# A fused two-layer kernel on Trainium2: one turn moved by a step, one normalisation moved ahead of a product, and the first gate given its own RMS factor

## The chip, the cores and the metric

The kernel runs on one core of a Trainium2 chip. One call computes both layers for all 32 batches. The metric is the device time of one call in microseconds (us). Each time comes from an execution on the chip; the profile is one further execution with the hardware profiler on.

## The reference, cut to what matters

x is 32 batches of 128 tokens with 128 features, all float32.

```python
# layer 0: RMS norm, gated MLP, 8-bit activations and ternary down weights
scale = cond @ norm_w.T + 1.0
ms = mean(x * x, -1)
h = x * (scale[:, None, :] * rsqrt(ms + 1e-6))
val, gate = split(h @ up_w.T, 2, -1)             # 512 each
h = val * gelu(gate)                             # exact gelu
y = act_quant(h) @ weight_quant(down_w).T
x = y + x
# layer 1: modulated attention (16 heads of 8) and modulated MLP
cond = silu(silu(t_embd @ W_t1.T + b_t1) @ W_t2.T + b_t2 + c_embd) @ W_c.T + b_c
g1, b1, g2, b2, a1, a2 = split(cond, 6, -1)
h = layernorm(x) * g1[:, None, :] + b1[:, None, :]
o = attention(h @ W_qkv.T + b_qkv) @ W_o.T + b_o
x = x + o * a1[:, None, :]
h = layernorm(x) * g2[:, None, :] + b2[:, None, :]
x = x + (gelu_tanh(h @ W_f1.T + b_f1) @ W_f2.T + b_f2) * a2[:, None, :]
```

## The kernel before, in words

The tokens of a batch lie on the 128 partitions, so one batch is a 128x128 tile of `x_tok`. Batches are taken in 8 groups of 4 (`GRP`). Nothing plans the order at run time: each engine's program is written out by hand, each engine takes its instructions in that order, and semaphores tie the engines together. Three stages follow each other and overlap at their seams.

- Stage A, `gated_mlp(s)`, is layer 0, one batch per step, with every engine a step or more behind the one before it. TensorE turns x (`transpose_x`), ScalarE multiplies the turned tile by the conditioning scale (`scale_x`, into `h0T`), TensorE makes the gate product and the val product (512 columns each), ScalarE takes Gelu with the RMS factor as its scale (`gate`, L772), VectorE multiplies val, RMS factor and gate (`hid`, L923). The RMS factor `rstd0` of four batches at once is made in two pieces: VectorE's `mean_squares` (`ms`, L870) and POOL's power -0.5 (`rms`, L1100). For the first group VectorE also makes the squares itself, at the start of its program: the first x comes in a load of its own, batches 1 to 3 in a second one. Then VectorE goes on to the weights of the down product: it sums |w| (`w_abs`, L879), TensorE adds the sums over the partitions (L286, 128x1), and four VectorE operations round the weights (`w_rnd`, `w_int`, `w_tern`, L887 to L891). `hid` of batch 0 is behind these in VectorE's order.
- Stage B, `attention(b)`, is the attention of one batch per step. In two halves of 8 heads TensorE makes scores (`exp_scores`), ScalarE exponentiates them (`exps`, L806), and TensorE weighs the values with the result (`weigh`). One step later VectorE turns the sums (`normalize`, `o_turn` L978, `rinv` L981), POOL divides (`scale_output`, `o_norm` L1190), VectorE turns the quotient back (`turn_back`, `feat` L985). In the last steps all exp scores use one pair of banks, so scores wait for the exp before them.
- Stage C, `mlp(i)`, is the output projection, the residual, the second layer norm and the MLP, one group per step. For a group: product with W_o (`output_projection`), VectorE's bias and gate (`gate_projection`, `projT`), the turn back to token rows (`residual`, L474), VectorE's addition into `x_tok` (`add_residual`, L999) and statistics (`statistics`, L1006 and L1010), POOL's `layer_norm` (`var_e`, `xc`, `rstd`, `xn`, L1196 to L1204), TensorE's turn of `xn` (`normalized_features`, L482), VectorE's `modulate` (`h2T`, L1017), four products with W_f1 each followed by ScalarE's Gelu (L845), and the product with W_f2.

The first pieces of stage C are put into the last attention steps. `FRONT` and `FRONT_END` (L87, L88) say which piece TensorE runs in which step: a piece of `FRONT` in the middle of the step, between the first weighing and the second scores, one of `FRONT_END` at its end. `FRONT_BANK` gives each its PSUM bank. Before, the turn of group 0's normalised rows ("norm", 0) is in the middle of step 30, the residual of group 1 ends step 30, the projection of group 2 ends step 31. Step 32 holds only what batch 31 still needs, and then `mlp(2)` begins, whose first products are the W_f1 products of group 0. VectorE's and POOL's counterparts are called from their own `attention(b)` (L1021) and `operand_parts(b)` (L1212): POOL runs `layer_norm(0)` at the end of step 29 and `layer_norm(1)` at the end of step 32, behind `scale_output(31)`.

Of the kernel before, what the change touches and what calls it, by code (L numbers as in the profile page):

```python
# [15 lines left out]
B = 32  # L16
D = 128
# [66 lines left out]

FRONT = {27: ("proj", 0), 28: ("res", 0), 29: ("proj", 1), 30: ("norm", 0)}  # L87
FRONT_END = {30: ("res", 1), 31: ("proj", 2)}  # L88
FRONT_BANK = {("proj", 0): 5, ("res", 0): 6, ("proj", 1): 5, ("norm", 0): 6, ("res", 1): 5, ("proj", 2): 7}
TWO_PAIRS = 27  # L90

# [58 lines left out]
def build(nc, x, first, early, late, cond, out):  # L150
    x_d = x.rearrange("b t d -> t b d")
    out_d = out.rearrange("b t d -> t b d")
    with ExitStack() as ctx:
# [232 lines left out]
        def _(pe):  # L386
# [114 lines left out]
            def attention(b):  # L501
                on, pre = 0 <= b < B, 0 <= b + LEAD < B
                if on:
                    exp_scores(b, 0)
                if 0 <= b - 1 < B:
                    weigh(b - 1, 1)
                if pre:
                    max_scores(b + LEAD, 0)
                if late_proj(b):
                    project(*late_proj(b))  # L510
                if b == LAST_LN:
                    transpose_last_ln()
                if b in FRONT:
                    front(*FRONT[b])
                if on:
                    exp_scores(b, 1)
                if on:
                    weigh(b, 0)
                if pre:
                    max_scores(b + LEAD, 1)  # L520
                if 0 <= b + LEAD - 1 < B:
                    transpose_max(b + LEAD - 1)
                if b in FRONT_END:
                    front(*FRONT_END[b])

            def transpose_x(b):
                if b == 0:
# [34 lines left out]
            keep_at_work(2)  # L562

            def gated_mlp(s):
                if s + 1 < B:
                    transpose_x(s + 1)
                if s < B:
                    n = s % 2
                    pe.wait_ge(a_h0T, s + 1)
                    if s == 0:  # L570
                        pe.wait_ge(up_gate_loaded, 32)
                    if s >= 2:
                        pe.wait_ge(a_gate, s - 1)
                    mm(bank(1 + n), h0T[:, n, :], we("up")[:, FF:2 * FF]).then_inc(a_gate_mm, 1)
                if s == 0:
                    pe.wait_ge(const_set, 6)
                    pe.wait_ge(wabs_set, 1)
                    pe.wait_ge(t2_set, 1)
                    mm(bank(MISC_BANK)[:, B:B + 1], ones[:, :], w_abs[:, :]).then_inc(wabs_mm, 1)
                if s == 1:  # L580
                    pe.wait_ge(wtern_set, 1)
                    pe.wait_ge(eye_b_set, 1)
                    for f in range(FC):
                        last = nc.tensor.transpose(bank(5).bitcast(BF16)[:, f * P:(f + 1) * P], w_tern[:, f * P:(f + 1) * P], eye_b[:, :])
                    last.then_inc(wternT_mm, 1)
                if s in EARLY_PROJ:
                    project(*EARLY_PROJ[s])
                if 0 <= s - 2 < B:
                    c, n = s - 2, s % 2
                    pe.wait_ge(a_hrnd, c + 1)  # L590
                    pe.wait_ge(a_hintT, c) if c else pe.wait_ge(wternT_set, 1)
                    low = hrnd[:, n, :].bitcast(BF16).rearrange("p (f two) -> p f two", two=2)
                    for f in range(FC):
                        last = nc.tensor.transpose(bank(5).bitcast(BF16)[:, f * P:(f + 1) * P], low[:, f * P:(f + 1) * P, 0], eye_b[:, :])  # L594
                    last.then_inc(a_hintT_mm, 1)
                if s < B:
                    n = s % 2
                    if s == 0:
                        pe.wait_ge(up_val_loaded, 16)
                    if s >= 2:  # L600
                        pe.wait_ge(a_hid, s - 1)
                    mm(bank(3 + n), h0T[:, n, :], we("up")[:, 0:FF]).then_inc(a_val_mm, 1)
                if s == 2:
                    pe.wait_ge(wstep_set, 1)
                    pe.wait_ge(c_set, 1)
                    pe.wait_ge(late_loaded, 16)
                    for n in range(6):
                        last = mm(bank(MISC_BANK)[:, n * B:(n + 1) * B], wl("cw")[:, n * D:(n + 1) * D], c_act[:, :])
                    last.then_inc(mods_mm, 1)
                if s == 4:  # L610
                    pe.wait_ge(mods_set, 6)
                    pe.wait_ge(perm_set, 3)
                    bq, bv = LATE_AT["b_q"][0], LATE_AT["b_v"][0]
                    mm(bank(MISC_BANK)[:, 0:2], eye_h[:, :], w_late[:, bq:bq + 2])
                    mm(bank(MISC_BANK)[:, 2:3], wl("wo"), w_late[:, bv:bv + 1]).then_inc(bias_mm, 1)
                if 0 <= s - 3 < B:
                    c, n = s - 3, (s - 3) % 2
                    pe.wait_ge(a_hintT, c + 1)
                    if c:
                        pe.wait_ge(a_x1, c)  # L620
                    for f in range(FC):
                        last = mm(bank(6)[:, 0:D], hintT[:, n, f, :], w_ternT[:, f, :], f == 0, f == FC - 1)
                    last.then_inc(a_y_mm, 1)
                if 0 <= s - LN_LAG < B and s < B:
                    transpose_ln(s - LN_LAG)
# [72 lines left out]
        def _(act):  # L698
# [61 lines left out]
                nc.scalar.copy(k_part[:, 0, :], k_f[:, :]).then_inc(k_cast, 1)  # L760

            def gated_mlp(s):
                if s + 1 < B:
                    scale_x(s + 1)
                if s < B:
                    n = s % 2
                    act.wait_ge(a_gate_mm, s + 1)
                    if s % GRP == 0:
                        act.wait_ge(rstd0_set, s // GRP + 1)
                    if s >= 2:  # L770
                        act.wait_ge(a_hid, s - 1)
                    nc.scalar.activation(gate[:, n, :], bank(1 + n), ACT.Gelu, scale=rstd0[:, s:s + 1]).then_inc(a_gate, 1)  # L772
                if s in EARLY_PROJ:
                    if s == 13:
                        act.wait_ge(bias_set, 2)
                    save_projection(*EARLY_PROJ[s])
# [72 lines left out]
        def _(dve):  # L849
# [8 lines left out]
            dve.wait_ge(first_loaded, 16)  # L858
            dve.wait_ge(t2_mm, 1)
            v.scalar_tensor_tensor(t2[:, :], bank(MISC_BANK)[:, 0:B], wf("b_t2"), wf("scale_fside"), ALU.add, ALU.add).then_inc(t2_set, 1)  # L860
            dve.wait_ge(x_first_loaded, 16)
            for b in range(GRP):
                if b == 1:
                    dve.wait_ge(x_loaded[0], 16)
                v.tensor_tensor_reduce(sq[:, b * D:(b + 1) * D], tile_cols(x_tok, b), tile_cols(x_tok, b), 1.0, 0.0,
                                       ALU.mult, ALU.add, ssq[:, b:b + 1]).then_inc(ssq_set, 1)
            dve.wait_ge(ssq_set, GRP)

            def mean_squares(g):
                v.tensor_scalar(ms[:, g * GRP:(g + 1) * GRP], ssq[:, g * GRP:(g + 1) * GRP], 1.0 / D, 1e-6,  # L870
                                ALU.mult, ALU.add).then_inc(ms_set, 1)

            mean_squares(0)
            v.tensor_copy(eye_b[:, :], eye).then_inc(eye_b_set, 1)
            dve.wait_ge(v_zero_set, 2)
            for at in ONES_AT:
# [23 lines left out]
            def gated_mlp(s):  # L900
# [47 lines left out]
                if s % GRP == 2 and s // GRP + 1 < NG:  # L948
                    g = s // GRP + 1
                    dve.wait_ge(sq_set, GRP * g)  # L950
                    mean_squares(g)
                if s == 3:
                    dve.wait_ge(mods_mm, 1)
                    dve.wait_ge(late_loaded, 16)
# [39 lines left out]
            def add_residual(g, n):  # L994
                xs = tile_cols(x_tok, GRP * g, GRP)
                dve.wait_ge(c_res_mm, g + 1)
                if g:
                    dve.wait_ge(c_xn, g)
                v.tensor_tensor(xs, bank(n), xs, ALU.add).then_inc(c_x2, 1)  # L999

            def statistics(g):
# [17 lines left out]
                last.then_inc(c_h2T, 1)  # L1019

            def attention(b):  # L1021
                if 0 <= b - 1 < B:
                    normalize(b - 1)
                if 0 <= b + LEAD < B:
# [9 lines left out]
                    maxima(b + LEAD, 1)  # L1034
                if b == 31:
                    statistics(1)
                if b == 32:
                    gate_projection(2, FRONT_BANK["proj", 2])
                if 0 <= b - 1 < B:
                    turn_back(b - 1)  # L1040
                if b == 28:
# [1 line left out]
                if b == 29:  # L1043
                    gate_projection(1, FRONT_BANK["proj", 1])
                if b == 30:
                    modulate(0, FRONT_BANK["norm", 0])
                    add_residual(1, FRONT_BANK["res", 1])

            for s in range(A_STEPS):
# [45 lines left out]
        def _(pool):  # L1095
            p = nc.gpsimd

            def rms(g):
                pool.wait_ge(ms_set, g + 1)
                p.tensor_tensor(rstd0[:, g * GRP:(g + 1) * GRP], ms[:, g * GRP:(g + 1) * GRP], half[:, :], ALU.pow).then_inc(rstd0_set, 1)  # L1100

            def by_half(to, of):
                view = of.rearrange("p (c j r f) -> p f c r j", c=DH, j=4, r=2, f=2)
# [39 lines left out]
            p.memset(q_st[0][:, :, :].rearrange("p h t -> p (h t)").bitcast(F32), 0.0).then_inc(stack_const_set, 1)  # L1143
            p.memset(v_pad[:, 1, :, :, :].rearrange("p s j c -> p (s j c)"), 0.0).then_inc(v_zero_set, 1)
            pool.wait_ge(const_set, 6)
            rms(0)

            def normalize_two(c):
                n, k = c % 4, c // 2
# [11 lines left out]
            def gated_mlp(s):  # L1161
# [5 lines left out]
                if s % 2 == 0 and 0 <= s - 6 < B - 2:  # L1167
                    normalize_two(s - 6)
                if s % GRP == 3 and s // GRP + 1 < NG:
                    rms(s // GRP + 1)  # L1170
                if s == 3:
                    pool.wait_ge(late_loaded, 16)
                    pool.wait_ge(first_loaded, 16)
# [38 lines left out]
            def operand_parts(b):  # L1212
                if b == 3:
                    normalize_two(B - 2)
                if b == 29:
                    layer_norm(0)
                if b == 32:
                    layer_norm(1)
                stage, g = b % GRP, (b + 8 - b % GRP) // GRP
                if b >= 0 and g < NG:  # L1220
# [47 lines left out]
```

## Time and profile before

| | |
|---|---|
| time, median of 3 runs | 308.49 us (307.62 to 309.13) |
| profiled execution, its own time | 306.38 us |
| its span, first to last instruction | 304.5 us |
| mean granted TensorE clock | 0.989 of full speed |
| TensorE, matmuls | busy 278.8 us, 92% of the span |
| TensorE, weight loads | 156.8 us, 51% |
| VectorE (DVE) | 241.2 us, 79% |
| ScalarE (ACT) | 188.6 us, 62% |
| GpSimd (POOL) | 175.0 us, 57% |

The engines work at the same time, so the shares don't add up to 100%. A float32 product is recorded as two instructions, each with a weight load (PEld). In the rows below, "[2.31 <-POOL xn L1204]" says that the engine stood idle for 2.31 us before this group of instructions, and that the last thing it waited for was POOL's `xn` of line 1204; "<-issue" stands for idle time in which it waited for nothing that the profile shows. Almost all of TensorE's products carry the line of one helper, L286, and are told apart by their tiles. Ends of matmuls are modelled, so the next start is the better mark.

### The profile page before, as it was taken

How to read it: one execution, taken by the hardware profiler on the slowest of the kernel's cores; microseconds unless marked ns; L12 is line 12 of the kernel's file. 1: busy time of each engine (PE TensorE's matmuls, PEld its weight loads, DVE VectorE, ACT ScalarE, POOL GpSimd, SP SyncE). 2: the span in 40 equal slices, each digit the busy share in tenths (PEclk: the TensorE clock that was granted, in tenths of full speed). 3: DMA queues.
4: the chain of work that ended last, by engine and by line, in shares of the span. 5: the costliest groups of instructions: out<-in, count | busy, mean ns of one | idle time of the engine just before them, and what ended most of it. 6: DMA issues, size and time to landing. Idle time of an engine off the chain costs nothing.

```text
span 304.5 us, 8273 instructions
## 1 busy us (share of the span) xinstructions
PE 278.8 (92%) x2918; PEld 156.8 (51%) x2918; DVE 241.2 (79%) x643; ACT 188.6 (62%) x355; POOL 175.0 (57%) x357
## 2 busy tenths in 40 slices
PE   8799999899889589989998999989869999999995
PEld 7355545444444336555656565656444445455444
DVE  4889999698789968888888888898975776676443
ACT  3666988888778448677877777776546222333330
POOL 7133576994996468895869596943344444322400
PEclk9999999999999959999999999999999999999999
DMA  7980000520440003435444444520000011011112
GB/s 197 341 159 4 0 3 11 142 67 0 111 107 0 0 8 99 132 86 144 108 123 122 107 122 108 156 76 6 6 4 2 0 34 37 5 31 34 36 34 71
DMA packets 26393, 21.58 MB, mean 71 GB/s; under 512 B 4432, under 2 KB 25840, under 8 KB 26096
## 3 DMA queue, kind: packets, MB, share of 16 engines
q1 hardware_dynamic: 25776, 20.24, 25.4%
q10 hardware_dynamic: 576, 0.80, 0.9%
q8 instruction: 24, 0.39, 0.5%
q14 instruction: 17, 0.14, 0.1%
HBM read 4.26 MB, written 2.10 MB: 21 GB/s over the span
## 4 chain that ended last, share of the span: by engine, by line
PE 56%; DVE 12%; POOL 11%; issue 9%; DMA 4%; ACT 4%; SPq 2%; DVEq 0%; POOLq 0%; ACTq 0%
PE psum L286 49%; DVE mx L971 4%; DMA q_st<-m_T 2%; DMA x_tok<-x 2%; DVE hid L923 2%; POOL q_rest L1110 2%; PE psum L594 1%; POOL q_part L1112 1%; PE psum L482 1%; ACT probs L806 1%; SPq L311 1%; DVE o_turn L978 1%; PE psum L675 1%; PE psum L474 1%; PE psum L538 1%
## 5 line engine op out<-in xcount | busy, mean ns | idle before, releaser
L971 DVE TENSOR_REDUCE mx<-psum 128x8 f32<-128x1024 f32 x64 | 75.5, 1192 | 13.4 <-PE psum L286 12.4
L806 ACT ACTIVATE probs<-psum 128x1024 f32<-128x1024 f32 x64 | 65.5, 1023 | 11.6 <-PE psum L286 10.4
L286 PE MATMUL psum<-w_early,h0T 128*128 128x512 f32 x128 | 67.2, 607 | 0.0
L845 ACT ACTIVATE g_act<-psum,w_late 128x512 f32<-128x512 f32 x32 | 22.0, 687 | 44.7 <-PE psum L286 44.7
L286 PE MATMUL psum<-probs,v_pad 128*32 128x128 f32 x1024 | 41.2, 278 | 2.8 <-DVE o_turn L978 1.8
L286 PE MATMUL psum<-h2T,w_late 128*128 128x512 f32 x64 | 31.4, 608 | 0.0
L286 PEld LDWEIGHTS psum<-probs,v_pad 128*32 128x32 f32 x1024 | 24.3, 109 | 10.8 <-ACT probs L806 4.4
L772 ACT ACTIVATE gate<-psum,rstd 128x512 f32<-128x512 f32 x32 | 22.0, 687 | 11.1 <-PE psum L286 5.8
L286 PE MATMUL psum<-g_act,w_late 128*128 128x512 f32 (+1 forms) x72 | 28.8, 545 | 0.0
L923 DVE SCALAR_TENSOR_TENSOR hid<-psum,rstd,gate 128x512 f32<-128x512 f32 x32 | 23.7, 742 | 5.0 <-ACT gate L772 2.6
L286 PE MATMUL psum<-q_st,k_st 64*128 64x128 bf16 x512 | 25.7, 220 | 2.1 <-DVE mx L971 0.7
L286 PE MATMUL psum<-k_st,q_st 64*128 64x128 bf16 x512 | 25.7, 222 | 1.9 <-DVE mx L971 1.9
L1158 POOL TENSOR_SCALAR xn_tile<-x_tok,mv,rstd 128x128 f32<-128x128 f32 x32 | 25.2, 795 | 1.7
L791 ACT ACTIVATE hrnd<-hid,qscale 128x512 f32<-128x512 f32 x32 | 22.9, 717 | 4.7 <-DVE qscale L947 4.3
L286 PEld LDWEIGHTS psum<-q_st,k_st 64*128 64x128 bf16 x512 | 14.8, 95 | 17.5 <-issue 11.4
L925 DVE TENSOR_REDUCE amax<-hid 128x1 f32<-128x512 f32 x32 | 22.0, 686 | 1.1
L286 PEld LDWEIGHTS psum<-k_st,q_st 64*128 64x128 bf16 x512 | 14.8, 95 | 15.4 <-issue 10.7
L1166 POOL TENSOR_TENSOR ystep<-qstep,w_step 128x1 f32<-128x1 f32 x32 | 6.1, 190 | 28.3 <-DVE qstep L935 28.3
L286 PEld LDWEIGHTS psum<-w_early,h0T 128*128 128x128 f32 x128 | 19.4, 192 | 0.6 <-issue 0.6
L594 PEld LDWEIGHTS psum<-eye_b,hrnd 128*128 128x128 bf16 x128 | 9.5, 98 | 19.4 <-issue 10.5
L1196 POOL TENSOR_TENSOR var_e<-mv,eps_c 128x4 f32<-128x4 f32 x8 | 1.6, 199 | 30.9 <-DVE mv L1010 30.9
L1134 POOL CAST m_part<-mx 128x16 bf16<-128x16 f32 x32 | 6.3, 197 | 21.9 <-DVE mx L971 21.9
(134 smaller groups left out, 557.5 us busy)
## 6 DMA issues: line engine op xcount, KB each, us to landing
q_st<-q_part SPq DMA_DIRECT2D x48, 128.0 KB
k_st<-k_part SPq DMA_DIRECT2D x48, 128.0 KB, 2.4
x_tok<-x SPq DMA_DIRECT2D x7, 256.0 KB, 8.0
out<-out_t SPq DMA_DIRECT2D x7, 256.0 KB, 2.3
w_late<-late SPq DMA_DIRECT2D x1, 1159.5 KB, 8.8
w_early<-early ACTq DMA_DIRECT2D x2, 256.0 KB, 5.5
k_st<-k_st SPq DMA_DIRECT2D x4, 128.0 KB, 6.2
q_st<-q_st SPq DMA_DIRECT2D x4, 128.0 KB
```

Of the source, the lines that this page charges most:

```text
L286: return nc.tensor.matmul(o, w, m, start=start, stop=stop, skip_group_check=shares)
L594: last = nc.tensor.transpose(bank(5).bitcast(BF16)[:, f * P:(f + 1) * P], low[:, f * P:(f + 1) * P, 0], eye_b[:, :])
L772: nc.scalar.activation(gate[:, n, :], bank(1 + n), ACT.Gelu, scale=rstd0[:, s:s + 1]).then_inc(a_gate, 1)
L791: nc.scalar.activation(hrnd[:, n, :], hid[:, n, :], ACT.Copy, bias=ROUND_UP, scale=qscale[:, c % 4:c % 4 + 1]).then_inc(a_hrnd, 1)
L806: nc.scalar.activation(probs[:, n % 3, :, :, :].rearrange("p f j q -> p (f j q)"), psum[:, pair[0]:pair[1] + 1, :].rearrange("p a b -> p ( ...
L845: nc.scalar.activation(g_act[:, f, :], bank(2 + f % 2), ACT.Gelu_apprx_tanh, bias=wl("b_f1")[:, f:f + 1]).then_inc(c_gelu[f], 1)
L923: v.scalar_tensor_tensor(hid[:, n, :], bank(3 + n), rstd0[:, s:s + 1], gate[:, n, :], ALU.mult, ALU.mult).then_inc(a_hid, 1)
L925: v.tensor_reduce(amax[:, m:m + 1], hid[:, n, :], X_AXIS, ALU.max, apply_absolute_value=True).then_inc(a_amax, 1)
L971: v.tensor_reduce(mx[:, c % 2, :, r, :], psum[:, pair[0]:pair[1] + 1, :].rearrange("p f (j k) -> p f j k", j=4), X_AXIS, ALU.max, negate=T ...
L1134: p.tensor_copy(parts[:, :, 0, :], m).then_inc(b_m, 1)
L1158: p.tensor_scalar(xn_tile[:, n + e, :], tile_cols(x_tok, c + e), mv[:, n + e, 0:1], rstd[:, n + e:n + e + 1], ALU.subtract, ALU.mult).then ...
L1166: p.tensor_tensor(ystep[:, c % 8:c % 8 + 1], qstep[:, c % 4:c % 4 + 1], w_step[:, :], ALU.mult).then_inc(a_ystep, 1)
```

## The change

The change has three parts.

1. Start. VectorE makes `ms` of batch 0 as soon as its own square is there, and of batches 1 to 3 later; POOL makes `rstd0` in the same two pieces. The gate of batch 0 waits for the first piece alone. On TensorE the turn of the second x, and on ScalarE its scaling, move behind the gate of batch 0.
2. Step 30. The turn of group 0's normalised rows moves from the middle of step 30 to the end of step 31, ahead of the third projection. VectorE's `modulate(0)` moves from step 30 to the start of step 32, and `gate_projection(2)` with it, ahead of `normalize(31)`. `add_residual` no longer waits for the `xn` of the group before.
3. Step 31. POOL's `layer_norm(1)` moves from the end of step 32 to the end of step 31, ahead of `scale_output(31)`.

```diff
-FRONT = {27: ("proj", 0), 28: ("res", 0), 29: ("proj", 1), 30: ("norm", 0)}
-FRONT_END = {30: ("res", 1), 31: ("proj", 2)}
+FRONT = {27: ("proj", 0), 28: ("res", 0), 29: ("proj", 1)}
+FRONT_END = {30: [("res", 1)], 31: [("norm", 0), ("proj", 2)]}
...
@@ TensorE @@
             def gated_mlp(s):
-                if s + 1 < B:
+                if 0 < s and s + 1 < B:
                     transpose_x(s + 1)
...
                     mm(bank(1 + n), h0T[:, n, :], we("up")[:, FF:2 * FF]).then_inc(a_gate_mm, 1)
+                if s == 0:
+                    transpose_x(1)
...
@@ ScalarE @@
             def gated_mlp(s):
-                if s + 1 < B:
+                if 0 < s and s + 1 < B:
                     scale_x(s + 1)
...
-                    if s % GRP == 0:
-                        act.wait_ge(rstd0_set, s // GRP + 1)
+                    if s < 2:
+                        act.wait_ge(rstd0_set, s + 1)
+                    elif s % GRP == 0:
+                        act.wait_ge(rstd0_set, s // GRP + 2)
...
+                if s == 0:
+                    scale_x(1)
...
@@ VectorE @@
             for b in range(GRP):
                 if b == 1:
+                    dve.wait_ge(ssq_set, 1)
+                    mean_squares(0, 1)
                     dve.wait_ge(x_loaded[0], 16)
...
-            mean_squares(0)
+            mean_squares(1, GRP)
...
             def add_residual(g, n):
...
                 dve.wait_ge(c_res_mm, g + 1)
-                if g:
-                    dve.wait_ge(c_xn, g)
...
             def attention(b):
+                if b == 32:
+                    modulate(0, FRONT_BANK["norm", 0])
+                    gate_projection(2, FRONT_BANK["proj", 2])
                 if 0 <= b - 1 < B:
                     normalize(b - 1)
...
-                if b == 32:
-                    gate_projection(2, FRONT_BANK["proj", 2])
                 if 0 <= b - 1 < B:
                     turn_back(b - 1)
...
                 if b == 30:
-                    modulate(0, FRONT_BANK["norm", 0])
                     add_residual(1, FRONT_BANK["res", 1])
...
@@ POOL @@
-            rms(0)
+            rms(1, 0, 1)
+            rms(2, 1, GRP)
...
             def operand_parts(b):
                 if b == 29:
                     layer_norm(0)
-                if b == 32:
+                if b == 31:
                     layer_norm(1)
```

`mean_squares(first, end)` and `rms(n, first, end)` are the old functions with the columns given by the caller; later groups call them with their four columns.

## Rows read from the trace of the kernel before

**Rows 1.** Stretches: PE, PEld, DVE, ACT, POOL busy (instructions), granted clock, DMA share, GB/s.

```profile
8.00:12.00 4.00, 3.09 (x10) 1.33 (x10) 3.09 (x16) 2.52 (x9) 1.02 (x1) 1.00 1.04 371
104.00:116.00 12.00, 9.99 (x114) 4.89 (x109) 8.84 (x16) 5.63 (x10) 6.89 (x17) 0.72 0.02 5
235.00:301.00 66.00, 65.73 (x216) 33.23 (x215) 41.83 (x141) 19.50 (x29) 19.16 (x24) 1.00 0.10 29
```

**Rows 2.** Timeline, 222 to 262 us: start, duration, engine, line, tiles, count, [idle before].

```profile
223.99 0.63 PE L482 MATMUL psum<-w_first,xn 128*128 128x128 f32 x4 [2.31 <-POOL xn L1204]
224.24 0.31 DVE L985 STREAM_TRANSPOSE feat<-o_norm 128x128 f32<-128x128 f32 x1 [1.42 <-POOL o_norm L1190]
224.65 1.36 DVE L1017 TENSOR_SCALAR h2T<-psum,mods 128x128 f32<-128x128 f32 x4
...
226.14 0.69 DVE L999 TENSOR_TENSOR x_tok<-psum,x_tok 128x512 f32<-128x512 f32 x1
...
227.67 0.40 PE L286 MATMUL psum<-q_st,k_st 64*128 64x128 bf16 x8 [0.54 <-ACT probs L806]
...
227.85 0.81 DVE L1006 BATCH_NORM_STATS2 stats<-x_tok 128x6 f32<-128x128 f32 x4
...
228.11 1.02 ACT L806 ACTIVATE probs<-psum 128x1024 f32<-128x1024 f32 x1 [0.49 <-PE psum L286]
...
228.57 1.13 PE L286 MATMUL psum<-feat,w_late 128*128 128x512 f32 x2
228.69 0.38 DVE L1010 BATCH_NORM_AGGREGATE mv<-stats 128x2 f32<-128x6 f32 x4
...
230.20 3.03 PE L286 MATMUL psum<-h2T,w_late 128*128 128x512 f32 x6
...
231.52 0.20 POOL L1196 TENSOR_TENSOR var_e<-mv,eps_c 128x4 f32<-128x4 f32 x1
...
233.50 1.02 PE L286 MATMUL psum<-h2T,w_late 128*128 128x512 f32 x2
233.75 1.04 POOL L1204 TENSOR_TENSOR xn<-xc,rstd 128x512 f32<-128x512 f32 x1
...
234.85 0.66 PE L482 MATMUL psum<-w_first,xn 128*128 128x128 f32 x4 [0.32 <-POOL xn L1204]
...
239.63 2.92 PE L286 MATMUL psum<-h2T,w_late 128*128 128x512 f32 x6
```

**Rows 3.** Timeline, 0 to 32 us: the first steps of stage A.

```profile
8.24 0.29 DVE L865 CUSTOM_DVE_ANT_0 sq<-x_tok 128x128 f32<-128x128 f32 x1 [2.14 <-DMA x_tok<-x]
...
8.44 1.02 PE L286 MATMUL psum<-w_early,h0T 128*128 128x512 f32 x2
8.47 0.20 ACT L722 ACTIVATE warm<-zero_c 128x1 f32<-128x1 f32 x1
...
9.32 1.02 POOL L1100 TENSOR_TENSOR rstd<-ms,half 128x4 f32<-128x4 f32 x1 [2.89 <-DVE ms L870]
...
10.10 0.35 PE L286 MATMUL psum<-w_abs,ones 128*128 128x1 f32 x2 [0.64 <-issue]
...
10.44 0.69 ACT L772 ACTIVATE gate<-psum,rstd 128x512 f32<-128x512 f32 x1 [1.43 <-POOL rstd L1100]
...
11.87 0.43 DVE L891 TENSOR_SCALAR w_tern<-w_int 128x512 bf16<-128x512 f32 x1
...
12.21 0.74 DVE L923 SCALAR_TENSOR_TENSOR hid<-psum,rstd,gate 128x512 f32<-128x512 f32 x1
```

**Rows 4.** Timeline, 207 to 224 us: the first half of attention step 30.

```profile
221.03 0.64 PE L286 MATMUL psum<-probs,v_pad 128*32 128x128 f32 x16
...
221.14 1.02 ACT L806 ACTIVATE probs<-psum 128x1024 f32<-128x1024 f32 x1
...
222.09 0.44 DVE L978 STREAM_TRANSPOSE o_turn<-psum 128x256 f32<-128x256 f32 x1
```

**Rows 5.** Chain of waits in order of time: start, duration, engine, tile, line, count.

```profile
252.22 0.86 PE psum L286 x2
```

More of the change, by code:

```diff
@@ L522, in attention @@
                     transpose_max(b + LEAD - 1)
-                if b in FRONT_END:
-                    front(*FRONT_END[b])
+                for kind, g in FRONT_END.get(b, []):
+                    front(kind, g)
             def transpose_x(b):
@@ L860, in _, with mean_squares @@
             v.scalar_tensor_tensor(t2[:, :], bank(MISC_BANK)[:, 0:B], wf("b_t2"), wf("scale_fside"), ALU.add, ALU.add).then_inc(t2_set, 1)
+            def mean_squares(first, end):
+                v.tensor_scalar(ms[:, first:end], ssq[:, first:end], 1.0 / D, 1e-6, ALU.mult, ALU.add).then_inc(ms_set, 1)
             dve.wait_ge(x_first_loaded, 16)
@@ L867, in _ @@
             dve.wait_ge(ssq_set, GRP)
-            def mean_squares(g):
-                v.tensor_scalar(ms[:, g * GRP:(g + 1) * GRP], ssq[:, g * GRP:(g + 1) * GRP], 1.0 / D, 1e-6,
-                                ALU.mult, ALU.add).then_inc(ms_set, 1)
-            mean_squares(0)
+            mean_squares(1, GRP)
             v.tensor_copy(eye_b[:, :], eye).then_inc(eye_b_set, 1)
@@ L950, in gated_mlp @@
                     dve.wait_ge(sq_set, GRP * g)
-                    mean_squares(g)
+                    mean_squares(GRP * g, GRP * g + GRP)
                 if s == 3:
@@ L1096, in _, with rms @@
             p = nc.gpsimd
-            def rms(g):
-                pool.wait_ge(ms_set, g + 1)
-                p.tensor_tensor(rstd0[:, g * GRP:(g + 1) * GRP], ms[:, g * GRP:(g + 1) * GRP], half[:, :], ALU.pow).then_inc(rstd0_set, 1)
+            def rms(n, first, end):
+                pool.wait_ge(ms_set, n)
+                p.tensor_tensor(rstd0[:, first:end], ms[:, first:end], half[:, 0:end - first], ALU.pow).then_inc(rstd0_set, 1)
             def by_half(to, of):
@@ L1169, in gated_mlp @@
                 if s % GRP == 3 and s // GRP + 1 < NG:
-                    rms(s // GRP + 1)
+                    g = s // GRP + 1
+                    rms(g + 2, GRP * g, GRP * g + GRP)
                 if s == 3:
```

## The prediction

> **What bounds the kernel now.** The stretches view comes first, because it says where a saved microsecond survives. In the row for 235 to 301 us TensorE is busy 65.73 of 66.00 us [rows 1]: from the first group's product with W_f2 to the last group it runs without a hole. Work that lets TensorE enter this stretch earlier moves the end by the same amount, as long as nothing inside the stretch begins to wait. Then the timeline of the hand-over from attention to the MLP: TensorE stands still for 2.31 us ahead of the turn of group 0 (L482), released by POOL's `xn` (L1204), and for 0.32 us ahead of the turn of group 1, released by the next `xn` [rows 2]. Last the timeline of the start, read for the wait that ends last ahead of batch 0's `hid` at 12.21: `gate` was over at 10.44 + 0.69 = 11.13, but VectorE itself was at `w_tern` from 11.87 to 12.30 [rows 3]. VectorE's order starts with the squares of the second x, for whose load it waited 2.14 us, and goes over the sum of |w| to `w_tern`. The start is bound by that order and not by the gate.
>
> **The change, part by part.**
>
> *Start: RMS factor of batch 0 alone, second x behind the gate.* Today batch 0's gate product follows the second x at 8.44, and its gate waits for `rstd`, which POOL gives at 9.32 + 1.02 = 10.34, behind all four squares [rows 3]. After the change the product waits for h0T of batch 0 and for the weights, both there before 8.44; I take 7.6, behind TensorE's filler products, so it ends by 8.7. VectorE's extra `ms` lies in its 2.14 us wait; behind that new wait (for batch 0's own square) only the wait for the second x is queued. POOL's `pow` on one column costs between nothing and the 1.02 us of four; I take 0.5, and either is over before the gate product. So batch 0's gate runs 8.7 to 9.4, right behind ScalarE's Gelu table (8.47 + 0.20), in place of 10.44 to 11.13. That is 1.7 us, or 0.9 if the product starts only at 8.44, and none of it counts: `hid` stands behind `w_tern` on VectorE and starts at 12.21. The second x turns at 8.7 and is scaled at 9.4 to 9.8; its own gate product stands on TensorE behind the sum of |w| at 10.10 and the val product of batch 0, and that cover would be gone only with a gate of batch 0 as late as today's. The factors of batches 1 to 3 start on POOL when today's four do (9.32) and cost between nothing and the same 1.02. Value 0; VectorE's order excludes a gain as long as `w_tern` is last.
>
> One rule speaks against this part. By the rows, TensorE's granted clock is 1.00 (2.4 GHz) from 8 to 12 us, with holes in it, and its only long fall towards 1.2 GHz lies in 104 to 116 us, 0.72 on the mean [rows 1]. Pulling the gate product forward lengthens the hole ahead of the sum of |w| from today's 0.64 us [rows 3] to about 1.4. The Trainium skill (TensorE: Matmul & The Clock Gate, "Part 1: The HAM clock gate") says that the throttled clock is the default, that activity releases it, and that the point of the change varies from run to run; by it a longer hole makes a fall likelier. By the row the cost is 0; with a fall as long as the one seen it is the fourth rival below.
>
> *Turn of group 0 one step later.* I follow TensorE with durations of [rows 2, 4]. A score product starts 0.06 us behind the exp that frees its banks; exp starts 0.44 behind the scores (227.67 to 228.11); scores and the weighing behind them take 0.90 from start to the next start (227.67 to 228.57), of which I give the scores 0.33; a turn takes 0.65.
> - Step 30: weigh(29) at 221.03 as today. With the turn gone from its place, scores(30, second) wait only for exp(30, first), 221.14 + 1.02 = 222.16, and start at 222.22 (today behind 223.99 + 0.63). weigh(30) needs `o_turn`, 222.09 + 0.44, and starts at 222.60. The residual of group 1 runs 223.17 to 223.83.
> - Step 31: exp(30, second) is 222.66 to 223.68, so scores(31, first) start at 223.87, exp 224.31 to 225.33, scores(31, second) 225.39, exp 225.83 to 226.85. On VectorE `feat` of batch 29 still waits for POOL and ends at 224.55; `x_tok` of group 1 comes straight behind it, since `modulate` is no longer between them and the wait for `c_xn` is gone: to 225.2. `o_turn` to 225.65 lets weigh(31, first) start at 225.72. Then the turn of group 0 is 226.3 to 226.95 (`xn` has been there since 223.84), the third projection lasts to 228.05, weigh(31, second) to 228.6.
> - VectorE beside it: `rinv` to 225.95, the statistics of group 1 with their aggregates 1.22 us (227.85 to 229.07), so to 227.17, `feat` of batch 30 to 227.4, modulate 1.36 us, to 228.75. The first product with W_f1 starts at 228.80 instead of 230.20. This is 1.40 us, and what is late next is VectorE's modulate, by 0.2 us.
>
> *Group 1 normalised ahead of the last product.* Today POOL starts group 1 at 231.52, behind `o_norm` of batch 31, and `xn` ends at 233.75 + 1.04 = 234.79: 3.27 us. After the change it starts when the statistics are over, about 227.25, and ends at 230.5. TensorE wants it behind the last W_f1 product, 0.86 us after its start [rows 5]: today 233.50 + 0.86 = 234.36, new 232.96. So the 0.49 us from 234.36 to 234.85 go too. Queued behind this normalisation on POOL is `o_norm` of batch 31, now done at 231.2; behind that, on VectorE, `feat` of batch 31 (231.5), `x_tok` of group 2, whose turn on TensorE ends at about 232.3 anyway, its statistics, and modulate of group 1, over at 235.5. The next group's first W_f1 product wants that at 239.63 - 1.9 = 237.7. So 2.2 us of slack remain, and the cost is 0.
>
> *The rest.* The removed waits for `c_xn` save only what is counted. projT of group 2 moves behind modulate, 228.75 to 230.05, and TensorE turns it behind three W_f1 products, 228.80 + 3.03 = 231.8: hidden by 1.7 us. ScalarE's table load for the MLP's Gelu moves with the last exp, 2.3 us forward (229.13 to 226.85), so it stays off the path. No DMA is issued or moved; SP's stores wait for outputs, which come earlier by the sum.
>
> **Sum.** 1.40 + 0.49 + 0 = 1.9 us at the entry of the full stretch. The profiled execution took 306.38 us (span 304.5) and would take 304.5. The three timed runs have a median of 308.49 (307.62 to 309.13), 2.1 above it; the same saving carried over gives 306.6. The forecast's own range is 305.8 to 307.4. A difference of 0.5%, 1.5 us, is about what a measurement of this kernel can tell from no change.
>
> **Rivals.**
> - *The hole comes back as a wait for VectorE.* TensorE now waits directly for a chain on VectorE in order: `x_tok`, `o_turn`, statistics, `feat`, modulate. For it: today `feat` of batch 29 stood 1.42 us behind POOL's `o_norm` [rows 2]; a smaller one, or 0.3 us on each of three steps, takes 0.9 from the 1.9 and leaves 1.0: 307.5. If all 1.4 of the entry come back, 0.5 is left: 308.0. Against it: POOL is idle when `o_norm` of batch 30 is due. Chance 0.31.
> - *The start pays as well*, because the first hid moves with its gate. For it: gate comes 1.7 us sooner. Against it: `w_tern` ends at 12.30 whatever gate does. It would give at most 12.21 - 11.13 = 1.1 more: 305.5. Chance 0.05.
> - *Slower: the last product is late.* `o_norm` of batch 31 stands behind the whole normalisation of group 1, and VectorE waits for it in order, ahead of x_tok, statistics and modulate of the MLP. It decides from the point where the slack of 2.2 us is used up, that is when group 1's statistics end past 229.4 rather than at 227.2; each further microsecond costs TensorE one at the next group's W_f1, and the later groups carry it on. With 3 us beyond the slack the time is 308.49 - 1.9 + 3 = 309.6. Against it: today these statistics ended at 229.07 with the hole of 2.31 us in front of them. Chance 0.03.
> - *Slower: TensorE's clock falls in the longer hole at the start.* The fall in 104 to 116 us lost (1 - 0.72) x 12 = 3.4 us of full clock [rows 1]. With all of it, 308.49 - 1.9 + 3.4 = 310.0; VectorE's chain would cover a part. Against it: the clock stays at 1.00 through today's holes at the start. Chance 0.05.
>
> **How the numbers follow.** The forecast has 0.56. Faster by over 0.5% takes most of it (0.50, since 1.9 lies only 0.4 above the bound), the start's 0.05 and a little of the first rival: 0.57. Within 0.5% is the rest of the forecast and of the first rival: 0.35. Slower is the two mishaps: 0.08. The range goes from the start paying in part, less a scatter of 0.7 as in the timed runs (305.2), to all of the entry coming back with some of that scatter (308.5).
>
> **What would show it.** Right: scores(30, second) 0.06 us behind exp(30, first); the turn of group 0 behind weigh(31, first), with no hole over 0.6 us at L482; the first W_f1 product some 7.8 us after weigh(29), not 9.2; no hole at the turn of group 1; gate of batch 0 at about 8.7 and yet hid at about 12.2. Wrong: a hole of over 0.5 us ahead of the first W_f1 product, released by VectorE's `h2T`; a hole within the MLP; hid earlier than the end of `w_tern`; a clock under 1.00 in the first 20 us.

## The result and the profile after

| | before | after |
|---|---|---|
| median of the first comparison | 307.66 us (15 runs) | 303.47 us (15 runs) |
| ratio, 95% interval | | 0.9864 (0.9828 to 0.990) |
| ratio in three later comparisons | | 0.9926 (0.9891 to 0.996), 0.9884 (0.9823 to 0.9945), 0.9885 (0.9823 to 0.9947) |
| profiled execution, span | 306.38, 304.5 | 302.25, 300.5 |

The changed kernel is faster by 4.2 us in the first comparison and by 2.3 to 3.6 us in the other three; the mean of the four is 3.4 us. Ratios and their intervals count only executions within 1.5% of the fastest of their kernel, medians count all. Forecast were 1.9 us and a range down to 305.2, so the time lies below the range.

The stretches of the changed kernel, to be laid beside [rows 1]; the last row is the same full stretch, taken 4 us earlier, as the turn of group 1 comes 4.00 us earlier, and the second the fall of TensorE's clock, shallower in this execution (0.86 against 0.72).

```profile
8.00:12.00 4.00, 3.77 (x10) 1.19 (x9) 3.33 (x17) 2.54 (x9) 0.87 (x1) 1.00 1.06 362
104.00:116.00 12.00, 9.73 (x137) 5.30 (x139) 9.85 (x18) 6.65 (x12) 7.52 (x21) 0.86 0.03 7
...
231.00:297.00 66.00, 65.68 (x217) 33.15 (x214) 41.22 (x140) 19.93 (x29) 19.17 (x24) 1.00 0.10 29
```

The timeline of its hand-over, to be laid beside [rows 2, 4].

```profile
219.25 0.65 PE L286 MATMUL psum<-probs,v_pad 128*32 128x128 f32 x16
219.36 1.02 ACT L812 ACTIVATE probs<-psum 128x1024 f32<-128x1024 f32 x1
...
220.44 0.40 PE L286 MATMUL psum<-q_st,k_st 64*128 64x128 bf16 x8 [0.55 <-ACT probs L812]
...
222.46 0.31 DVE L993 STREAM_TRANSPOSE feat<-o_norm 128x128 f32<-128x128 f32 x1 [1.42 <-POOL o_norm L1198]
...
222.69 0.65 DVE L1005 TENSOR_TENSOR x_tok<-psum,x_tok 128x512 f32<-128x512 f32 x1
223.27 0.43 DVE L986 STREAM_TRANSPOSE o_turn<-psum 128x256 f32<-128x256 f32 x1
...
223.90 0.81 DVE L1012 BATCH_NORM_STATS2 stats<-x_tok 128x6 f32<-128x128 f32 x4
...
224.48 0.66 PE L482 MATMUL psum<-w_first,xn 128*128 128x128 f32 x4
...
225.24 1.32 DVE L1023 TENSOR_SCALAR h2T<-psum,mods 128x128 f32<-128x128 f32 x4
...
226.72 3.00 PE L286 MATMUL psum<-h2T,w_late 128*128 128x512 f32 x6
...
227.44 1.04 POOL L1212 TENSOR_TENSOR xn<-xc,rstd 128x512 f32<-128x512 f32 x1
...
229.99 1.02 PE L286 MATMUL psum<-h2T,w_late 128*128 128x512 f32 x2
...
230.85 0.60 PE L482 MATMUL psum<-w_first,xn 128*128 128x128 f32 x4
```

Both holes ahead of L482 are gone. From weigh(29), the second weighing of batch 29 in step 30, to the turn of group 1 it takes 230.85 - 219.25 = 11.60 us; before, 234.85 - 221.03 = 13.82. That is 2.22 us. The other 1.78 of the 4.0 us between the two spans were there at weigh(29) already (221.03 against 219.25), before anything in the hand-over runs: 0.35 come from the start, and 1.43 from between `hid` of batch 0 and weigh(29) (208.82 against 207.39 us), where the clock fell. The section on the experiments lays that stretch beside the clock in all traces.

The timeline of its start, to be laid beside [rows 3].

```profile
7.39 1.91 PE L286 MATMUL psum<-w_early,h0T 128*128 128x512 f32 x2
7.90 0.29 DVE L877 CUSTOM_DVE_ANT_0 sq<-x_tok 128x128 f32<-128x128 f32 x1 [1.60 <-DMA x_tok<-x]
...
9.35 0.69 ACT L776 ACTIVATE gate<-psum,rstd 128x512 f32<-128x512 f32 x1 [0.68 <-PE psum L286]
9.72 0.30 PEld L286 LDWEIGHTS psum<-w_abs,ones 128*128 128x128 f32 x2 [1.24 <-issue]
...
11.52 0.43 DVE L899 TENSOR_SCALAR w_tern<-w_int 128x512 bf16<-128x512 f32 x1
11.86 0.75 DVE L931 SCALAR_TENSOR_TENSOR hid<-psum,rstd,gate 128x512 f32<-128x512 f32 x1
```

The gate comes 1.1 us sooner (9.35 against 10.44), and `hid` comes 3.96 us after the square of the second x, as before (12.21 - 8.24 = 3.97). The 0.35 us come from the load, which landed sooner in this execution.

### The profile page after: what moved, and what is told of

Same layout as the page of the kernel before. It is cut to its first block, busy times and chain, and to the rows that moved or that the text cites. A ratio compares the mean times of both kernels' runs of the same rounds, so it can differ in the third digit from the quotient of the medians.

```text
span 300.5 us, 8269 instructions
## 1 busy us (share of the span) xinstructions
PE 277.8 (92%) x2918; PEld 156.7 (52%) x2918; DVE 240.8 (80%) x644; ACT 188.4 (63%) x355; POOL 175.6 (58%) x358
## 4 chain that ended last, share of the span: by engine, by line
PE 60%; DVE 15%; POOL 10%; issue 9%; ACT 3%; DMA 1%; SPq 1%; DVEq 0%; POOLq 0%; ACTq 0%
PE psum L286 53%; DVE mx L979 5%; DVE hid L931 2%; POOL q_rest L1116 2%; PE psum L596 1%; POOL q_part L1118 1%; DVE o_turn L986 1%; DMA q_st<-m_T 1%; PE psum L482 1%; PE psum L677 1%; PE psum L474 1%; PE psum L538 1%; PE psum L533 1%; PE psum L448 1%; POOL q_part L1122 1%
## 5 line engine op out<-in xcount | busy, mean ns | idle before, releaser
L286 PE MATMUL psum<-w_early,h0T 128*128 128x512 f32 x128 | 68.0, 614 | 0.0
L286 PEld LDWEIGHTS psum<-w_ternT,hintT 128*128 128x128 bf16 x128 | 9.6, 99 | 17.6 <-issue 17.1
```

Of the source, the lines that this page charges most:

```text
L286: return nc.tensor.matmul(o, w, m, start=start, stop=stop, skip_group_check=shares)
```

## The experiments

Theory A: the hand-over pays 2.2 us, the start nothing, the rest is scatter between executions. Theory B: the start pays as well. Theory C came with the first results: the hole costs more than its waiting, because TensorE's clock falls in it in part of the executions. The path is, from here on, the time from weigh(29) to the turn of group 1.

**One part at a time.** `e1_handover_only` takes the start back, `e2_start_only` takes the hand-over back, `e3_turn_only` takes only the move of the normalisation back, `c1_changed_again` is the changed kernel on the same chip.

```diff
# e1, against the changed kernel
-                if 0 < s and s + 1 < B:
+                if s + 1 < B:
                     transpose_x(s + 1)
...
-                    mean_squares(0, 1)
...
-            rms(1, 0, 1)
-            rms(2, 1, GRP)
+            rms(1, 0, GRP)
# e2, against the changed kernel
-FRONT = {27: ("proj", 0), 28: ("res", 0), 29: ("proj", 1)}
+FRONT = {27: ("proj", 0), 28: ("res", 0), 29: ("proj", 1), 30: ("norm", 0)}
-FRONT_END = {30: [("res", 1)], 31: [("norm", 0), ("proj", 2)]}
+FRONT_END = {30: [("res", 1)], 31: [("proj", 2)]}
...
# e3, against the changed kernel (also in e2)
-                if b == 31:
+                if b == 32:
                     layer_norm(1)
```

> The changed kernel with the start as it was before (one RMS factor for the group, second x ahead of the gate). Theory A (the start pays nothing, the hand-over pays 2.2 us, what is above that between the two sets of runs is scatter of the second x's load and of the stretch at 1.2 GHz around 104 to 113 us): 2.2 us faster than the kernel before, ratio about 0.993, and not to be told from the changed kernel. Theory B (the start pays about 2 us besides, by a way not yet seen): ratio about 0.993 as well, but some 2 us slower than the changed kernel. In the profile, by both: 11.6 us from weigh(29) to the turn of group 1, against 13.8 before.

Measured: 303.83 us, ratio 0.9894 (0.9858 to 0.993); the changed kernel beside it 303.87. weigh(29) to the turn of group 1: 232.73 - 221.13 = 11.60 us. Taking the start back shows no cost: against theory B.

> The kernel before with the changed start alone. Theory A: within 0.5 us of the kernel before, ratio 0.999 to 1.001; hid of batch 0 starts about 4.0 us after the squares of the second x, as in both kernels. Theory B: about 2 us faster, ratio 0.993.

Measured: 307.81 us, ratio 1.0009 (0.9982 to 1.0036). The start alone shows no gain, and the 0.993 of theory B lies outside the interval. Its timeline has the gate at 9.02 and `hid` still 3.96 us behind the square (8.19 to 12.15):

```profile
8.19 0.29 DVE L877 CUSTOM_DVE_ANT_0 sq<-x_tok 128x128 f32<-128x128 f32 x1 [1.89 <-DMA x_tok<-x]
...
9.02 0.69 ACT L776 ACTIVATE gate<-psum,rstd 128x512 f32<-128x512 f32 x1 [0.35 <-PE psum L286]
...
12.15 0.75 DVE L931 SCALAR_TENSOR_TENSOR hid<-psum,rstd,gate 128x512 f32<-128x512 f32 x1
```

But its hand-over, which is that of the kernel before, took 233.77 - 218.06 = 15.71 us in this execution, 1.89 more than in the execution of [rows 2]. The stretches and the timeline show why: TensorE's clock fell in the 2.31 us hole, and the products behind it, weighing among them (1.08 instead of 0.65 us), ran at 1.2 GHz.

```profile
218.00:222.00 4.00, 1.69 (x26) 1.09 (x20) 2.12 (x7) 1.12 (x2) 3.15 (x4) 0.77 0.02 4
222.00:226.00 4.00, 4.00 (x53) 2.60 (x52) 2.06 (x5) 1.75 (x2) 0.00 (x0) 0.50 0.02 4
```

```profile
218.06 0.65 PE L286 MATMUL psum<-probs,v_pad 128*32 128x128 f32 x16
221.01 1.09 PE L482 MATMUL psum<-w_first,xn 128*128 128x128 f32 x4 [2.31 <-POOL xn L1214]
222.57 1.08 PE L286 MATMUL psum<-probs,v_pad 128*32 128x128 f32 x16
...
233.77 0.66 PE L482 MATMUL psum<-w_first,xn 128*128 128x128 f32 x4 [0.32 <-POOL xn L1214]
```

> The changed kernel with the normalisation of group 1 back in step 32, behind the last product. The first W_f1 product still starts 7.5 us after weigh(29), but the rinv of batch 31 comes only behind modulate and the projection on VectorE, so POOL starts group 1 some 3.8 us later than in the changed kernel and TensorE waits about 1.4 us at the turn of group 1: 13.0 us from weigh(29) to that turn, 1.4 us slower than the changed kernel. A rival (the two edits are independent, each worth its own term of 1.40 and 0.49) would have 12.1 us and 0.5 us.

Measured: 304.7 us, ratio 0.9924 (0.9896 to 0.9953); 235.06 - 222.05 = 13.01 us from weigh(29) to the turn of group 1, 1.41 more than in the changed kernel, as forecast; the medians differ by 0.8 us. The two edits are not independent: with the turn late, modulate and the projection stand ahead of batch 31's `rinv` on VectorE, and POOL's normalisation behind `o_norm` becomes TensorE's wait:

```profile
231.03 0.25 DVE L989 RECIPROCAL rinv<-o_turn 128x16 f32<-128x16 f32 x1
231.36 0.41 POOL L1198 TENSOR_TENSOR o_norm<-o_turn,rinv 128x128 f32<-128x128 f32 x1 [4.09 <-DVE rinv L989]
...
233.96 1.04 POOL L1212 TENSOR_TENSOR xn<-xc,rstd 128x512 f32<-128x512 f32 x1
...
235.06 0.65 PE L482 MATMUL psum<-w_first,xn 128*128 128x128 f32 x4 [1.25 <-POOL xn L1212]
```

> The changed kernel once more, as the measure for the other three on the same chip: ratio 0.983 to 0.990 if the first comparison was not a chance of its runs; 0.993 if only the 2.2 us of the hand-over are the change's.

Measured: 303.87 us, ratio 0.9926. The same two kernels gave 0.9864 in the first comparison: the two differ by 1.9 us, so neither number alone settles whether 2.2 us are all.

**The clock in each execution.** Every execution, but for those of the kernel before in the first comparison, comes with its mean granted clock. Of those that the ratios count, 23 of 54 were at or under 0.981 for the kernels that have the 2.31 us hole as it was (before, `e2`), and 1 of 48 for those without it (the changed kernel four times, `e1`, `e3`); of all executions, `e4` with the former, 41 of 72 and 2 of 53. The mean is a rough sign only, since it also holds the fall at 104 to 116 us. In the traces that fall alone took the mean no lower than 0.983 (`e1`, `e3`, `c3`), and the execution of `e2` above, whose clock fell in the hole and not there, has 0.987. Theory C asks for a test in which the wait stays and TensorE does not stand still.

**The hole filled.**

```diff
# e5, against the kernel before
                 if (kind, g) == ("norm", 0):
                     pe.wait_ge(c_x2, 1)
+                    for _ in range(9):
+                        mm(bank(n)[:, 0:P], ones[:, :], ones[:, :])
```

> The kernel before with nine 128-column products of constants on TensorE (0.22 us each, some 1.9 us) in the 2.31 us hole ahead of the turn of group 0; their result is used nowhere. The hole's wait stays: 13.8 us from weigh(29) to the turn of group 1 at full clock. Theory C (the saving is 2.2 us of waiting and, besides, the falls to 1.2 GHz that the hole brings on in part of the executions: mean granted clock under 0.982 in 11 of 25 runs of the kernel before, in none of 29 without the hole): no execution under 0.981, and 0.5 to 1.2 us faster than the kernel before, ratio 0.996 to 0.998. Theory A (what is above 2.2 us is scatter): the clocks are as in the kernel before, ratio 0.999 to 1.002.

Measured: 305.45 us, ratio 0.9952 (0.9912 to 0.9992); the lowest of 12 clocks is 0.983. The wait is still there, 233.96 - 220.20 = 13.76 us to the turn of group 1:

```profile
220.20 0.64 PE L286 MATMUL psum<-probs,v_pad 128*32 128x128 f32 x16
220.78 2.27 PE L286 MATMUL psum<-ones 128*128 128x128 f32 x18
223.07 0.66 PE L482 MATMUL psum<-w_first,xn 128*128 128x128 f32 x4
...
233.96 0.66 PE L482 MATMUL psum<-w_first,xn 128*128 128x128 f32 x4 [0.33 <-POOL xn L1206]
```

Products that compute nothing make the kernel before faster, by 1.5 us (0.2 to 2.7) against the 0.5 to 1.2 expected. The wait is as long as before and the low clocks are gone, so what they save is the clock behind the hole. This is as theory C has it; theory A's unchanged clocks did not come.

**The normalisation alone.** `e4` is the kernel before with the one line of `e3` the other way round.

> The kernel before with the normalisation of group 1 in step 31 alone, the turn of group 0 left in step 30. The statistics of group 1 end 8.0 us after weigh(29) as before, so POOL starts at once and xn is ready 11.4 us after weigh(29) in place of 13.8; TensorE's turn of group 1 comes 13.3 us after weigh(29), 0.5 less than before, bound by the W_f1 products. A rival (the last product, now behind the normalisation, holds VectorE) would show the turn at 13.8 or later, or a hole at the next group's W_f1.

Measured: one execution, 306.28 us. The clock fell in its hole too (the turn of group 0 took 1.09 us), so the turn of group 1 came 234.80 - 219.65 = 15.15 us after weigh(29), and the 13.3 could not be seen. What can be seen is the second half: the turn stands 0.86 us behind the last W_f1 product and waits for nothing, 234.80 - 230.63 = 4.17 us behind the first one against 234.85 - 230.20 = 4.65. That is the 0.49 us of the forecast.

```profile
222.53 1.09 PE L482 MATMUL psum<-w_first,xn 128*128 128x128 f32 x4 [2.23 <-POOL xn L1204]
...
230.63 3.03 PE L286 MATMUL psum<-h2T,w_late 128*128 128x512 f32 x6
...
233.94 1.02 PE L286 MATMUL psum<-h2T,w_late 128*128 128x512 f32 x2
234.80 0.60 PE L482 MATMUL psum<-w_first,xn 128*128 128x128 f32 x4
```

**The seam of stage A and attention filled as well.** The seam is the stretch at 98 to 116 us, in whose second part [rows 1] shows a low clock. `e6` and `e8` are one kernel, the changed one with thirteen products of constants at five places of the seam (2, 3, 3, 1 and 4); `e7` is the kernel before with these and those of `e5`.

```diff
+            def fillers(n):
+                for _ in range(n):
+                    mm(bank(AV_BANK)[:, 2 * P:3 * P], ones[:, :], ones[:, :], shares=True)
...
+                    if b == -2:
+                        fillers(2)
                     max_scores(b + LEAD, 0)
...
+                if s == 32:
+                    fillers(4)
```

> The changed kernel with thirteen such products in TensorE's waits at the seam of stage A and attention (98 to 106 us), where the clock falls in all but a few executions; their result is used nowhere. By theory C, taken over to this seam: mean clock 0.998 to 1.000 in most executions, and by the line through all runs so far (143 us for a clock of 1, so 0.8 us for each 0.0056) 1.4 us faster than the changed kernel: 302.2, ratio to the kernel before 0.985. Rival (VectorE and POOL set the pace of this seam, so TensorE's clock there costs nothing, or the products themselves delay the work behind them): clock up, time unchanged within 0.3 us or longer.

> The changed kernel once more on the same chip as the measure for the filled seam: 303.5 to 303.9, ratio 0.987 to 0.993, mean clock between 0.982 and 1.000.

Measured: `e6` 302.06 us, ratio 0.9863 (0.9808 to 0.9919), clocks 0.993 to 1.000; the changed kernel beside it 303.06, ratio 0.9884, clocks 0.982 to 0.999. The stretch of [rows 1] in `e6` has the full clock, and its product for q takes 1.10 us, against 2.05 in the kernel before:

```profile
104.00:116.00 12.00, 10.23 (x158) 6.01 (x152) 10.91 (x20) 7.44 (x13) 8.84 (x23) 1.00 0.05 13
```

```profile
102.92 0.94 PE L286 MATMUL psum<-ones 128*128 128x128 f32 x6
...
106.61 1.10 PE L286 MATMUL psum<-feat,wq_h 128*128 128x512 f32 x2
```

> The kernel before with both sets of products of constants, in the hole ahead of the turn of group 0 and at the seam of stage A and attention; their results are used nowhere. Theory C: the clock is 0.998 or more in nearly all executions, the scatter shrinks to about 1 us, and what is left between this kernel and the changed kernel with the seam filled is the waiting alone: 2.2 us. By theory A with a real saving of 3 to 4 us in the waits, the difference would be 3 us or more.

> The changed kernel with the seam filled, once more: about 302.0, 2.2 us under the kernel before with both places filled, 0.5 to 1.4 us under the changed kernel.

> The changed kernel on the same chip: 303.0 to 303.9, clock between 0.982 and 1.000.

Measured: `e7` 304.5 us (12 runs, 10 of them at a clock of 0.999 or 1.000), `e8` 302.4, the changed kernel 303.26. Counted as the ratios are, `e7` has a median of 304.24 and the twelve runs of `e6` and `e8` together 302.34: 1.9 us apart (95% interval 1.1 to 3.1, by redrawing the runs; 2.16 with all runs). With the clock held up on both sides, this is what the 2.2 us of waiting would leave, and the 3 us or more of theory A lie at the edge of the interval. The traces are sharper: from `hid` of batch 0 to weigh(29) the three executions take 207.1 to 207.3 us, and on the path 233.56 - 219.80 = 13.76 us in `e7` against 230.92 - 219.33 = 11.59 in `e6` and 11.60 in `e8`.

```profile
219.80 0.64 PE L286 MATMUL psum<-probs,v_pad 128*32 128x128 f32 x16
220.37 2.27 PE L286 MATMUL psum<-ones 128*128 128x128 f32 x18
...
233.56 0.65 PE L486 MATMUL psum<-w_first,xn 128*128 128x128 f32 x4 [0.33 <-POOL xn L1220]
```

Two expectations were missed. The scatter did not shrink to 1 us: the ten runs of `e7` at 0.999 or more lie between 302.85 and 305.21, and those of `e8` at 0.998 or more between 301.59 and 305.62, so 2 to 4 us of spread are there with the clock held, and their cause is open. And the filled seam is not shown to be faster than the changed kernel: counted as the ratios are, 302.34 against 303.37 for the changed kernel's runs, 1.0 us (-0.1 to 1.7), with the ratios 0.9863 and 0.9884 on one chip and 0.9896 and 0.9885 on the other. The rival that the products delay the work behind them has the traces for it, as the next paragraph shows.

**All thirteen traces, cut in three.** From the turn of group 1 to the end every execution takes 69.6 to 69.7 us, so whatever is gained ahead of that turn is kept, as the prediction had it. On the path it is 11.6 us in all seven traces that have both hand-over edits, 13.0 in `e3`, 13.8 in those of the kernel before whose clock held (before, `e5`, `e7`), and 15.15 and 15.71 in `e4` and `e2`, whose clock fell in the hole. From `hid` of batch 0 to weigh(29) the time goes with the granted clock in 104 to 120 us, and not with the change:

| clock in 104 to 120 us | traces | us from `hid` to weigh(29) |
|---|---|---|
| 0.68 | `e1`, `e3`, `c3` | 209.3 to 209.9 |
| 0.79 | before, `e5`, `c1`, `c2` | 208.2 to 208.8 |
| 0.89 | changed, `e4` | 207.4 to 207.7 |
| 1.00 | `e2` | 205.9 |
| 1.00, seam filled | `e6`, `e7`, `e8` | 207.1 to 207.3 |

So the fall at the seam costs up to some 4 us in an execution, and the filled seam takes 1.2 to 1.4 us more than the one execution whose clock held there without products.

## Why the prediction was wrong

- *Start: value 0.* Right, and for the reason given: in the kernel before, the changed one, `e1` and `e2`, `hid` of batch 0 comes 3.96 or 3.97 us behind the square of the second x, whenever the gate is done. The gate came later than worked out (9.35 for 8.7), because its product took 1.91 us and not 1.02; in `c1`, where it took 1.03, the gate was at 8.57.
- *Turn of group 0: 1.40 us.* The mechanism was right, the size too small. Measured from weigh(29): scores(30, second) at 1.19 as forecast, the turn of group 0 at 5.23 (forecast 5.27), the first W_f1 product at 7.47 (forecast 7.77; before 9.17), so 1.70. The 0.3 us were lost in the sum on VectorE, where each instruction was put behind the end of the one before it; in the rows the next starts before that end (`o_turn` at 223.27, while `x_tok` runs to 223.34; `h2T` at 225.24, while `feat` runs to 225.32).
- *Group 1 ahead of the last product: 0.49 us.* Right, 0.52: 4.65 us from the first W_f1 product to the turn before, 4.13 after, 4.17 in `e4`. The slack behind it was there: modulate of group 1 ended at 233.45, the next group's W_f1 began at 235.58.
- *Sum: 1.9 us.* On the path it is 2.22, by the traces; `e7` against `e6` and `e8`, with 1.9 us (1.1 to 3.1), agrees. The failed step is the one behind the sum, "the same saving carried over": it puts what the 2.31 us hole does to TensorE's clock at nothing, without a reason. The profiled execution of the kernel before held its clock at 2.4 GHz through the hole, and the sum was made as if all executions did. In `e2` and `e4` the hole let it fall, which made the path 1.9 us longer than before in `e2`, and filling the hole gave 1.5 us (0.2 to 2.7). With the 2.2 that is 3.7; the four comparisons have 3.4 on the mean. An estimate from the counts, 1.9 us in 23 of 54 executions, gives the clock 0.8 us and the whole 3.0. Both fit, so the clock's share is known only roughly, as 0.8 to 1.5 us.
- *What it was taken from.* The forecast of 306.6 also started too high: 308.49 is the median of three runs, and the fifteen of the first comparison have 307.66. Of the 3.1 us between 306.6 and 303.47 this is 0.8, the path 0.3, and the other 2.0 the clock behind the hole and scatter together.
- *The rule on the clock.* The rule of the Trainium skill (TensorE: Matmul & The Clock Gate, "Part 1: The HAM clock gate") was laid against the change, at a hole of 1.4 us at the start, and not for it, at the larger hole which the change takes away. The Trainium skill's sentence that activity releases the throttle agrees with `e5`, where TensorE at work in the hole kept the clock. That the point varies from run to run, which the Trainium skill says of the rise, agrees with the start (7.40 to 9.51 us, last section); for the fall it is shown by the hole itself, in which the clock held in the kernel before and fell in `e2`.
- The first comparison's 4.2 us hold about 0.8 more than the mean of the four; between the two traces the 1.43 us ahead of weigh(29) go with the fall at 104 to 116 us, shallower after. Nothing in the experiments ties that to the change.
- *Rivals.* The hole came back as a wait for VectorE of 0.15 us only (`e8`, ahead of the first W_f1 product); the start did not pay; the last product was not late. The clock did not fall in the start's longer hole: in `c1` it is 1.35 us long, and the val product behind it took 1.10 us as before. The changed kernel's profiled execution can't show this, since its slow gate product left a hole of only 0.23 us.

```profile
7.39 1.03 PE L286 MATMUL psum<-w_early,h0T 128*128 128x512 f32 x2
...
9.89 0.35 PE L286 MATMUL psum<-w_abs,ones 128*128 128x1 f32 x2 [1.35 <-issue]
10.10 1.10 PE L286 MATMUL psum<-w_early,h0T 128*128 128x512 f32 x2
```

## What to carry to other kernels

This hole on TensorE cost its length and, in part of the executions, the half-speed stretch behind it; look at the granted clock of many executions, not only at the one that was profiled. Before a hole's saving is summed from one trace, fill the hole with products that compute nothing: what that alone gains is the clock's share, and what removing the wait gains on top is the path's. The products themselves can cost time, as at the seam, so check in the trace that the work behind them starts when it did. And moving one edit of a pair can make the other necessary: the late turn without the early normalisation lost 1.4 of the 2.2 us again.

## What the hardware showed that was not expected

The same pair of gate products, started at 7.39 us, took 1.91 us in one execution of the changed kernel, 1.59 in `e2` and 1.03 in `c1`, while the profile's rows give a granted clock of 1.00 there.

```profile
7.39 1.59 PE L286 MATMUL psum<-w_early,h0T 128*128 128x512 f32 x2
```

The clock records kept with the traces begin, at full clock, at 9.51 us in the first of these executions, at 8.53 in `e2` and at 7.40 in `c1`, and hold nothing ahead of that; the row shows 1.00 where there is no record. So TensorE was still coming up from 1.2 GHz at that point of the start, at a moment that differs between executions, and the row did not show it; the duration of a known product did.
